# Order of the three matmuls in a block: high weights by low x first, instead of high weights by high x

## The chip, the cores and the metric

The kernel runs on one core of a Trainium2 chip. The metric is the device time of one execution in microseconds (us); lower is better. Before the change the median of three runs is 2578.09 us (2578.03 to 2578.33).

## The reference

The input x has 128 batch elements of 128 channels and 2048 positions (float32). Four layers follow each other, each added to its own input:

```
x = x + conv(x, W0) + (c @ cw0.T)[:, :, None] + side[None, :, None]     # 4 groups, 9 taps, padding 4
x = x + einsum('boi,bih->boh', agg_w1, x) + agg_b1[:, :, None]          # 1x1, weights mixed per batch element
x = x + einsum('boi,bih->boh', agg_w2, x) + agg_b2[:, :, None]          # the same with other experts
x = x + conv(x, W3) + (c @ cw3.T)[:, :, None] + side[None, :, None]     # 4 groups, 9 taps, padding 4
```

Here c is a condition vector of 128 numbers per batch element. For the second and third layer agg_w and agg_b are sums over 8 experts, weighted with a softmax that a small network (two gelu layers) makes of c.

## The kernel before

**Layout.** In a convolution the 2048 positions are cut into 4 phases (PH) of 512 (N). The rows of a tile are then the 32 channels of a group by the 4 phases, and there is one such tile for each of 4 groups (G). Nine taps over 4 phases become BLK = 3 matrices of 128x128, a band with the residual already added on its diagonal. A group of output is thus three column offsets m = 0, 1, 2 of the padded x, each against its own matrix. The two middle layers are joined: their two 128x128 matrices, with their residuals, are multiplied once per batch element (line 917, `middle_matrix`, the short matmuls named `pair<-mixed`), and the product is applied to x in channel rows, phase by phase (`middle`, line 927).

**High and low halves.** float32 accuracy is reached with operands of type float32r in three matmuls. Each operand is split in a rounded high part and the remainder, low. The product is high weights by high x, high weights by low x, low weights by high x, all added in PSUM. I call these three a block. A block stands in `conv` for each (group, m), so 12 blocks for each convolution and batch element, and in `middle` for each phase q, so 4. With two convolutions that makes 28 blocks, 84 big matmuls, for a batch element. The weights of the convolutions (w_hi, w_lo) are made once; m_hi and m_lo are made for each batch element.

**Who makes what.** SyncE issues every transfer in the loop: loads, stores, and the moves between channel rows and phase rows (x_ch, x_ph). ScalarE cuts x in phases, rounds it to x_hi, evacuates PSUM with the bias added (lines 484, 493, 503) and joins the output. VectorE mixes the experts (line 701), makes m_hi and m_lo, and makes the low halves: line 661 for the x of the next batch element, line 752 for the input of the last convolution, group by group (`split_x3`), line 737 for the middle, phase by phase (`split_x1`); lines 654 and 779 do so for the first two elements.

**Order of the work.** Every engine has its order written out by hand. TensorE's loop body for batch element b is `middle_matrix(b)`, `conv1(b)`, `conv4(b - 1)`, `middle(b)`. All waits on semaphores stand ahead of a group (in `conv1` and `conv4`) or of a phase (in `middle`): for the low half of x, which is made after the high half, and for the PSUM bank, which must have been evacuated. Only the last matmul of a group or phase increments a semaphore, with its low weights. The profile's names leave the numbers of tiles out: `x_hi` stands for x_hi, x3_hi and x1_hi, `w_hi` for both layers' weights.

Of the kernel before, what the change touches and what calls it, by code (L numbers as in the profile page):

```python
# [5 lines left out]
def cond_resid_kernel(nc: bass.Bass, a, out):  # L6
# [50 lines left out]
    with ctx:  # L57
        def sb(name, shape, dt=f32):
            return ctx.enter_context(nc.sbuf_tensor(name, shape, dt))
# [12 lines left out]
        x1_hi = sb("x1_hi", [C, PH, N], f32r)  # L72
        x1_lo = sb("x1_lo", [C, PH, N], f32r)
# [11 lines left out]
        w_hi = [sb(f"w_hi{l}", [C, BLK, G, C], f32r) for l in range(2)]  # L85
        w_lo = [sb(f"w_lo{l}", [C, BLK, G, C], f32r) for l in range(2)]
# [6 lines left out]
        m_hi = sb("m_hi", [C, C], f32r)  # L93
        m_lo = sb("m_lo", [C, C], f32r)
# [138 lines left out]
        def wait(eng, s, value):  # L233

            if not (isinstance(value, int) and value <= 0):
                eng.wait_ge(s, value)
# [590 lines left out]
        def _(pe):  # L827
# [23 lines left out]
            for l in range(2):  # L851
# [3 lines left out]
                                 stop=True).then_inc(score_done, 1)  # L855
# [6 lines left out]
            for l in range(2):  # L862
                pe.wait_ge(att_t_ready, l + 1)
                nc.tensor.matmul(bank[2 + l][:, 0:B], bias_k[:, l, :], att_t[l][:, :], start=True,
                                 stop=True).then_inc(bias_l_done, 1)
# [7 lines left out]

            def conv(l, g, hi, lo, done):
                for m in range(BLK):
                    for w, x in ((w_hi, hi), (w_hi, lo), (w_lo, hi)):
                        mm = nc.tensor.matmul(conv_bank[g % 2], w[l][:, m, g, :], x[:, g, m:m + N],  # L877
                                              start=(m == 0 and x is hi and w is w_hi),
                                              stop=(m == BLK - 1 and w is w_lo))
                mm.then_inc(done, 1)  # L880

            def conv1(b, groups=range(G)):
                if not isinstance(b, int) or b >= 2:
                    pe.wait_ge(x_lo_ready, b - 1)
                for g in groups:

                    if isinstance(b, int) and b == 0:
                        pe.wait_ge(x_lo_first, g + 1)
                    if isinstance(b, int) and b == 1:
                        pe.wait_ge(x_lo_second, g + 1)  # L890
                    if g >= 2:
                        pe.wait_ge(x1_ready, G * b + g - 1)
                    elif isinstance(b, int) and b == 1:
                        pe.wait_ge(x1_ready, g + 3)
                    elif not isinstance(b, int) or b >= 2:
                        pe.wait_ge(x4_ready, G * (b - 2) + g + 3)
                    conv(0, g, x_hi, x_lo, conv1_done)

            def conv4(b, groups=range(G), after_x4=False):
                for g in groups:  # L900

                    pe.wait_ge(x3_split, G * b + g + 1)

                    if g >= 2:
                        pe.wait_ge(x4_ready, G * b + g - 1)
                    elif after_x4:
                        pe.wait_ge(x4_ready, G * (b - 1) + g + 3)
                    else:
                        pe.wait_ge(x1_ready, G * (b + 1) + g + 3)
                    conv(1, g, x3_hi, x3_lo, conv4_done)  # L910
# [9 lines left out]
            def middle(b):  # L920

                wait(pe, x3_ready, 2 * b)
                pe.wait_ge(m_split, 2 * b + 2)
                for q in range(PH):
                    pe.wait_ge(x1_split, PH * b + q + 1)
                    for m, x in ((m_hi, x1_hi), (m_hi, x1_lo), (m_lo, x1_hi)):
                        mm = nc.tensor.matmul(mid_bank[:, q, :], m[:, :], x[:, q, :],  # L927
                                              start=(m is m_hi and x is x1_hi), stop=(m is m_lo))
                    mm.then_inc(mid_done, 1)

            def step(b):
                middle_matrix(b)
                conv1(b)
                conv4(b - 1)
                middle(b)
# [18 lines left out]
                             stop=True).then_inc(bias3_done, 1)  # L954

            middle(0)
            conv1(1)
            middle_matrix(1)
            pe.wait_ge(w4_lo_ready, PH)
            conv4(0)  # L960
            middle(1)
            with pe.Fori(2, B - 1) as b:
                step(b)
# [46 lines left out]
```

## Time and profile before

| | |
|---|---|
| median of 3 runs | 2578.09 us |
| the profiled execution, its own time | 2577.78 us |
| its span, first to last instruction | 2575.7 us |
| mean granted TensorE clock | 0.997 |
| TensorE busy, matmuls | 2550.1 us, 99%, 11,068 instructions |
| TensorE weight loads, beside the matmuls | 2069.8 us, 80%, 11,068 |
| VectorE busy | 1955.4 us, 76% |
| ScalarE busy | 2100.5 us, 82% |
| GpSimd busy | 16.1 us, 1% |
| DMA, mean | 314 GB/s |

A busy share says how long an engine had work in it; for TensorE matmuls overlap, each is shown longer than the distance to the next one, so its spacing is read from the starts. The span and the profiled execution's own time differ by what lies around the first and last instruction. The chain that ended last is followed back from the last instruction to what released each piece of work.

### The profile page before, as it was taken

The page shows a single profiled execution, that of the slowest core. Times are in us where ns is not written, and L with a number is a line of the kernel's source. Part 1 is how long each engine was busy: PE and PEld are TensorE (multiplying, and loading weights), DVE is VectorE, ACT ScalarE, POOL GpSimd, SP SyncE. Part 2 cuts the span into 40 slices and gives each one's busy share as a digit, 9 for nine tenths or more (in the row PEclk, how much of TensorE's full clock was granted, in tenths as well). Part 3 has the DMA queues.
Part 4 walks back from the last instruction along what each step waited for, and adds up shares of the span by engine and source line. Part 5 has one row for each costly group of instructions (what it writes and reads, how often), then busy time and mean ns, then how long its engine had stood idle before and what let it go on. Part 6 is the DMA issues. An engine that isn't in the chain of part 4 may idle for free.

```text
span 2575.7 us, 42996 instructions
## 1 busy us (share of the span) xinstructions
PE 2550.1 (99%) x11068; PEld 2069.8 (80%) x11068; DVE 1955.4 (76%) x5032; ACT 2100.5 (82%) x1937; POOL 16.1 (1%) x29
## 2 busy tenths in 40 slices
PE   8999999999999999999999999999999999999998
PEld 6888888888888888888888888888888888888886
DVE  8777777777777777777777777777777777777774
ACT  6888888888888888888888888888888888888885
POOL 2000000000000000000000000000000000000000
PEclk9999999999999999999999999999999999999999
DMA  7888888888888888888888888888888888888876
GB/s 254 316 320 317 318 319 319 315 318 323 318 312 321 323 318 313 320 324 316 315 320 323 315 317 319 322 317 316 320 320 317 317 319 319 316 318 322 317 297 237
DMA packets 334986, 809.31 MB, mean 314 GB/s; under 512 B 37370, under 2 KB 39426, under 8 KB 302210
## 3 DMA queue, kind: packets, MB, share of 16 engines
q1 hardware_dynamic: 332736, 807.69, 84.3%
q10 hardware_dynamic: 2242, 1.53, 0.2%
q8 instruction: 3, 0.05, 0.0%
q14 instruction: 5, 0.04, 0.0%
HBM read 137.97 MB, written 134.23 MB: 106 GB/s over the span
## 4 chain that ended last, share of the span: by engine, by line
PE 98%; DMA 1%; DVE 1%; ACT 0%; SPq 0%; issue 0%; DVEq 0%; ACTq 0%
PE pair L877 82%; PE quad L927 14%; PE pair L917 1%; DMA x_ch<-x_ph 0%; DVE partial L701 0%; DMA mix<-att_saved 0%; DMA x_ph<-in_small 0%; SPq L269 0%; SPq L321 0%; SPq L294 0%; DMA att_saved<-att 0%; ACT x_out L569 0%; ACT x_ch L422 0%; DVE x_hi L734 0%; ACT x_ph L575 0%
## 5 line engine op out<-in xcount | busy, mean ns | idle before, releaser
L877 PE MATMUL pair<-x_hi,w_hi 128*128 128x512 f32 x3072 | 1227.7, 400 | 2.9 <-DVE x_lo L752 1.2
L877 PE MATMUL pair<-x_hi,w_lo 128*128 128x512 f32 x3072 | 1213.5, 395 | 0.0
L877 PE MATMUL pair<-x_lo,w_hi 128*128 128x512 f32 x3072 | 1209.2, 394 | 0.0
L877 PEld LDWEIGHTS pair<-x_hi,w_lo 128*128 128x128 f32 x3072 | 579.7, 189 | 137.5
L877 PEld LDWEIGHTS pair<-x_lo,w_hi 128*128 128x128 f32 x3072 | 582.0, 189 | 131.7
L877 PEld LDWEIGHTS pair<-x_hi,w_hi 128*128 128x128 f32 x3072 | 579.0, 188 | 131.3 <-DVE x_lo L752 1.6
L484 ACT ACTIVATE x_ph<-pair,bias_now 128x512 f32<-128x512 f32 x512 | 351.2, 686 | 254.8 <-PE pair L877 254.7
L422 ACT COPY x_ch<-x_in 128x1024 f32<-128x1024 f32 x255 | 528.3, 2072 | 0.0
L475 ACT COPY x_out<-x_ch 128x1024 f32<-128x1024 f32 x252 | 517.3, 2053 | 0.0
L493 ACT ACTIVATE x_ph<-pair,bias_now 128x512 f32<-128x512 f32 x508 | 355.5, 700 | 191.3 <-PE pair L877 191.3
L734 DVE CAST x_hi<-x_ch 128x512 fp32r<-128x512 f32 x512 | 204.9, 421 | 325.9 <-DMA x_ch<-x_ph 325.9
L701 DVE SCALAR_TENSOR_TENSOR partial<-expert,mix,partial 128x128 f32<-128x128 f32 x1536 | 416.8, 347 | 0.0
L752 DVE TENSOR_TENSOR x_lo<-x_ph,x_hi 128x512 fp32r<-128x512 f32 x512 | 339.9, 684 | 0.0
L737 DVE TENSOR_TENSOR x_lo<-x_ch,x_hi 128x512 fp32r<-128x512 f32 x512 | 339.5, 683 | 0.0
L661 DVE TENSOR_TENSOR x_lo<-x_ph,x_hi 128x2048 fp32r<-128x2048 f32 x126 | 287.6, 2283 | 0.0
L503 ACT ACTIVATE x_ch<-quad,bias_now 128x1024 f32<-128x1024 f32 x256 | 275.4, 1134 | 7.9 <-PE quad L927 7.9
L430 ACT CAST x_hi<-x_ph 128x2048 fp32r<-128x2048 f32 x126 | 239.1, 1898 | 0.0
L748 DVE CAST x_hi<-x_ph 128x512 fp32r<-128x512 f32 x512 | 204.4, 420 | 8.3 <-DMA x_ph<-x_ch 8.1
L927 PE MATMUL quad<-x_hi,m_hi 128*128 128x512 f32 x512 | 203.1, 397 | 2.4 <-DVE x_lo L737 2.4
L927 PE MATMUL quad<-x_hi,m_lo 128*128 128x512 f32 x512 | 203.4, 397 | 0.0
L927 PE MATMUL quad<-x_lo,m_hi 128*128 128x512 f32 x512 | 202.8, 396 | 0.0
L759 DVE TENSOR_SCALAR bias_now<-bias 128x4 f32 (+1 forms) x127 | 21.6, 170 | 150.3 <-ACT x_ph L493 150.3
(83 smaller groups left out, 772.9 us busy)
## 6 DMA issues: line engine op xcount, KB each, us to landing
x_ph<-x_ch SPq DMA_DIRECT2D x1024, 256.0 KB, 2.5
x_ch<-x_ph SPq DMA_DIRECT2D x1024, 256.0 KB, 2.6
x_in<-in_x SPq DMA_DIRECT2D x128, 1024.0 KB, 5.6
out<-x_out SPq DMA_DIRECT2D x128, 1024.0 KB, 4.3
x_out<-in_W SPq DMA_DIRECT2D x8, 144.0 KB, 3.9
expert<-in_e ACTq DMA_DIRECT2D x2, 512.0 KB, 8.1
mix<-att_saved SPq DMA_DIRECT2D x2, 512.0 KB, 6.3
x_ph<-in_small ACTq DMA_DIRECT2D x1, 458.5 KB, 3.4
```

The lines of the kernel that those rows point to most:

```text
L422: nc.scalar.copy(x_ch[:, phases, :], x_in[:, slot, :].rearrange("c (n p) -> c p n", p=PH)[:, phases, :]).then_inc(x_cut, 1)
L430: nc.scalar.copy(x_hi[:, :, HALO:N + HALO], x_ph[:, :, :]).then_inc(x_hi_ready, 1)
L475: nc.scalar.copy(x_out[:, slot, :].rearrange("c (n p) -> c p n", p=PH)[:, phases, :], x4_ch[:, phases, :]).then_inc(x_joined, 1)
L484: nc.scalar.activation(x1_ph[:, g, :], conv_bank[g % 2], ACT.Identity, bias=bias1_now[:, g:g + 1]).then_inc(x1_ready, 1)
L493: nc.scalar.activation(x4_ph[:, g, :], conv_bank[g % 2], ACT.Identity, bias=bias4_now[:, g:g + 1]).then_inc(x4_ready, 1)
L503: nc.scalar.activation(x3_ch[:, phases, :], mid_bank[:, phases, :], ACT.Identity, bias=bias3_now[:, :]).then_inc(x3_ready, 1)
L661: nc.vector.tensor_tensor(x_lo[:, :, HALO:N + HALO], x_ph[:, :, :], x_hi[:, :, HALO:N + HALO].bitcast(f32), ALU.subtract).then_inc(x_lo_re ...
L701: nc.vector.scalar_tensor_tensor(to, term, mix[l][:, b, k:k + 1], of, ALU.mult, ALU.add).then_inc(mix_ready[l], 1)
L737: nc.vector.tensor_tensor(x1_lo[:, q - 1, :], x1_ch[:, q - 1, :], x1_hi[:, q - 1, :].bitcast(f32), ALU.subtract).then_inc(x1_split, 1)
L752: nc.vector.tensor_tensor(x3_lo[:, g - 1, HALO:N + HALO], x3_ph[:, g - 1, :], x3_hi[:, g - 1, HALO:N + HALO].bitcast(f32), ALU.subtract).t ...
L877: mm = nc.tensor.matmul(conv_bank[g % 2], w[l][:, m, g, :], x[:, g, m:m + N], start=(m == 0 and x is hi and w is w_hi), stop=(m == BLK - 1 ...
L927: mm = nc.tensor.matmul(mid_bank[:, q, :], m[:, :], x[:, q, :], start=(m is m_hi and x is x1_hi), stop=(m is m_lo))
```

## The change

In both places where a block is issued, the first two of its three matmuls change places. The flag that starts the accumulation goes to the new first matmul, and the last one (low weights by high x, with the increment) is as before. Nothing else is edited.

```
 for m in range(BLK):
-    for w, x in ((w_hi, hi), (w_hi, lo), (w_lo, hi)):
+    for w, x in ((w_hi, lo), (w_hi, hi), (w_lo, hi)):
         mm = nc.tensor.matmul(conv_bank[g % 2], w[l][:, m, g, :], x[:, g, m:m + N],
-                              start=(m == 0 and x is hi and w is w_hi),
+                              start=(m == 0 and x is lo),
                               stop=(m == BLK - 1 and w is w_lo))
...
 for q in range(PH):
     pe.wait_ge(x1_split, PH * b + q + 1)
-    for m, x in ((m_hi, x1_hi), (m_hi, x1_lo), (m_lo, x1_hi)):
+    for m, x in ((m_hi, x1_lo), (m_hi, x1_hi), (m_lo, x1_hi)):
         mm = nc.tensor.matmul(mid_bank[:, q, :], m[:, :], x[:, q, :],
-                              start=(m is m_hi and x is x1_hi), stop=(m is m_lo))
+                              start=(x is x1_lo), stop=(m is m_lo))
```

## Rows read from the trace of the kernel before

**Rows 1.** The page, busy time, share of the span and instructions per engine.
```profile
PE 2550.1 (99%) x11068; PEld 2069.8 (80%) x11068; DVE 1955.4 (76%) x5032; ACT 2100.5 (82%) x1937; POOL 16.1 (1%) x29
```

**Rows 2.** The page, chain that ended last, by engine and by line.
```profile
PE 98%; DMA 1%; DVE 1%; ACT 0%; SPq 0%; issue 0%; DVEq 0%; ACTq 0%
PE pair L877 82%; PE quad L927 14%; PE pair L917 1%; DMA x_ch<-x_ph 0%; DVE partial L701 0%; DMA mix<-att_saved 0%; DMA x_ph<-in_small 0%; SPq L269 0%; SPq L321 0%; SPq L294 0%; DMA att_saved<-att 0%; ACT x_out L569 0%; ACT x_ch L422 0%; DVE x_hi L734 0%; ACT x_ph L575 0%
```

**Rows 3.** The chain in order of time, 400 to 460 us: start, length, what.
```profile
436.02 2.79 PE quad L927 x12
438.81 0.22 PE pair L917 x2
439.03 16.75 PE pair L877 x72
```

**Rows 4.** The chain's longest pieces over the whole span, first and last steady one.
```profile
419.27 16.75 PE pair L877 x72
...
2494.07 16.75 PE pair L877 x72
```

**Rows 5.** Stretches: length, busy us (instructions), clock, DMA share, GB/s.
```profile
0.00:60.00 60.00, 47.19 (x183) 38.42 (x184) 48.28 (x122) 34.53 (x43) 16.14 (x29) 0.91 0.74 264
...
500.00:1000.00 500.00, 500.00 (x2177) 406.23 (x2176) 383.79 (x996) 414.96 (x380) 0.00 (x0) 1.00 0.86 319
...
38.00:43.00 5.00, 5.00 (x12) 3.89 (x13) 5.00 (x12) 1.11 (x1) 0.00 (x0) 0.50 0.02 3
```

**Rows 6.** Groups of instructions: TensorE's weight loads, one kind of line 877.
```profile
L877 PEld LDWEIGHTS pair<-x_lo,w_hi 128*128 128x128 f32 x3072 | 582.0, 189 | 131.7
```

**Rows 7.** VectorE's instructions in order of time, 990 to 1012 us.
```profile
1004.50 0.68 DVE L737 TENSOR_TENSOR x_lo<-x_ch,x_hi 128x512 fp32r<-128x512 f32 x1
...
1007.65 2.28 DVE L661 TENSOR_TENSOR x_lo<-x_ph,x_hi 128x2048 fp32r<-128x2048 f32 x1
```

**Rows 8.** Instructions of TensorE in order of time, 1008.5 to 1013 us.
```profile
1008.90 0.39 PE L927 MATMUL quad<-x_hi,m_hi 128*128 128x512 f32 x1
...
1011.83 0.47 PE L877 MATMUL pair<-x_hi,w_hi 128*128 128x512 f32 x1
...
1012.14 0.39 PE L877 MATMUL pair<-x_lo,w_hi 128*128 128x512 f32 x1
1012.14 0.19 PEld L877 LDWEIGHTS pair<-x_hi,w_lo 128*128 128x128 f32 x1
1012.37 0.39 PE L877 MATMUL pair<-x_hi,w_lo 128*128 128x512 f32 x1
```

**Rows 9.** Waits of TensorE: us in total, times, longest.
```profile
PE quad L927 <- DVE x_lo L737: 2.4, 2, 1.9
PE pair L877 <- DVE x_lo L752: 1.2, 1, 1.2
PE pair L877 <- DVE x_lo L654: 1.2, 1, 1.2
```

**Rows 10.** Groups of matmuls, 60 to 2500 us: count, busy us, mean ns, idle before.
```profile
L877 PE MATMUL pair<-x_hi,w_hi 128*128 128x512 f32 x2961 | 1181.7, 399 | 0.0
L877 PE MATMUL pair<-x_hi,w_lo 128*128 128x512 f32 x2962 | 1169.0, 395 | 0.0
L877 PE MATMUL pair<-x_lo,w_hi 128*128 128x512 f32 x2962 | 1165.0, 393 | 0.0
L927 PE MATMUL quad<-x_hi,m_lo 128*128 128x512 f32 x496 | 196.2, 396 | 0.0
L927 PE MATMUL quad<-x_lo,m_hi 128*128 128x512 f32 x496 | 195.5, 394 | 0.0
L927 PE MATMUL quad<-x_hi,m_hi 128*128 128x512 f32 x496 | 195.4, 394 | 0.0
```

**Rows 11.** TensorE in order of time, first element's middle, 38 to 43 us.
```profile
38.36 0.63 PE L927 MATMUL quad<-x_lo,m_hi 128*128 128x512 f32 x1
...
42.20 0.63 PE L927 MATMUL quad<-x_lo,m_hi 128*128 128x512 f32 x1
```

## The prediction

> **What bounds the kernel now.** I read the page's busy shares first: TensorE is busy 99% of the span of 2575.7 us, ScalarE 82%, VectorE 76% [rows 1]. The reader should distrust such a share until the chain agrees, so the chain that ended last comes next: 98% of it is TensorE, 82% on the convolutions' line 877, 14% on the middle layers' line 927 and 1% on the matrix product of line 917 [rows 2]. Third, the chain in order of time. In steady state it has three kinds of piece for one batch element and no other: 72 matmuls in 16.75 us, 12 in 2.79 us, 2 in 0.22 us [rows 3]. That is 19.76 us, and the pattern repeats without a drift: from the piece at 419.27 us to the one at 2494.07 us there are 105 batch elements in 2074.80 us, 19.760 us each [rows 4]. No DMA, no ScalarE and no VectorE stands in between.
>
> So the time is a count times a spacing. Per element there are 84 big matmuls (128x512); (16.75 + 2.79) / 84 gives 232.6 ns from one start to the next. The spacing is the same in both places: 16.75 / 72 = 232.6 ns in the convolutions, 2.79 / 12 = 232.5 ns in the middle [rows 3]. Over 128 elements, 84 x 128 = 10,752 matmuls x 0.2326 us = 2501 us, and 128 x 0.22 = 28 us for line 917. The other 47 us of the span are the first and last elements' waits and the start at half clock. The granted clock is 1.00 (the level of 2.4 GHz) in the steady stretch and 0.91 on average in the first 60 us [rows 5].
>
> **The change part by part.** Nothing is removed or added. Within each block of three matmuls the first two change places, in conv 3072 times, in middle 512 times, 3584 blocks in all.
>
> *Count of matmuls and weight loads: 0 us.* The weights run high, high, low in either order, only the moving operand goes from high, low, high to low, high, high. The trace loads weights once for each matmul, also for the second of two that use the same w_hi: 3072 loads on line 877 for the kind shown, and as many for each of the other two [rows 6]; line 927 has 512 of each. There is no skipped reload to lose or to win; 3 x 3584 loads stand on both sides. The loads take 189 ns on average beside a matmul that starts 233 ns before the next one, so they are covered by the stream. Were that cover gone, 189 ns would be to pay per matmul, but the edit lengthens no load.
>
> *The waits: 0 us, and the bound is small.* The first matmul of a block now needs the low half of x, which VectorE makes last. Had the old order let the high matmul start before the low half was there, the change would expose that. It did not: in conv1, conv4 and middle every wait stands ahead of the whole group, and it already is a wait for the low half (x_lo_ready, x3_split, x1_split). Behind it on TensorE is the same group as before. In steady state it binds nowhere. VectorE's line 737 makes the middle's first low phase from 1004.50 to 1005.18 us; TensorE starts the middle at 1008.90, 3.7 us later. Line 661 ends the next element's low x at 1007.65 + 2.28 = 1009.93; conv1 starts at 1011.83, 1.9 us later [rows 7, 8]. TensorE's waits for a low half over the whole trace are 2.4 + 1.2 + 1.2 = 4.8 us, at the two ends [rows 9]. Price 0; the far bound is that these double, +4.8 us, though no instruction that would do it is moved.
>
> *The start flag, the end of a group, the buffers: 0 us.* The start flag moves with the first place. The last matmul is still w_lo by the high x and carries the increment, so evacuations, moves by DMA and the release of x_hi and x_lo come at the same distance from the group's start as before. A third of each block stays where it was; no DMA is issued from TensorE and no queue is passed.
>
> *The pairing of what streams with what is loaded: the one unknown.* Each weight load runs while the matmul before it streams. The rows show it: the load for w_lo starts at 1012.14, in the same hundredth as the matmul with x_lo [rows 8]. Before, high x streams beside a load of w_hi, low x beside w_lo, high x beside the next w_hi. After, low x streams beside w_hi, high x beside w_lo, high x beside the next w_hi. If a step costs something for what streams plus something for what is loaded, the sum over a block is unchanged, since both sets stay (x high, high, low; weights high, high, low). Only an interaction of the two can move the time, and the trace has just the old pairs. Nearest rows: the mean durations of the three kinds between 60 and 2500 us. In conv they are 399, 393 and 395 ns, in the middle 394, 394 and 396 [rows 10]. The 399 holds one matmul in 24 that runs 0.47 us, the first behind line 917, whose two short matmuls leave the next load uncovered [rows 8]; without it the mean is 399 - (470 - 395) / 24 = 396. So the kinds differ by 3 ns in conv and 2 ns in the middle, with another kind the longest. A difference that doesn't stay with the kind doesn't look like a price of a pair. I take 0. For the far bounds one step in each block gains or loses the whole 3 ns: 3584 x 0.003 = 10.8 us either way. For the range I take a third of it, 1 ns per block: 3.6 us.
>
> There is something left to explain in each step. From 38 to 43 us the granted clock is 0.50, the level of 1.2 GHz [rows 5], and nine steps of the middle of the first element take 42.20 - 38.36 = 3.84 us, 426.7 ns each [rows 11]: 512 columns at 1.2 GHz and no more. The same columns at 2.4 GHz are 213.3 ns, but the spacing there is 232.6, 19.3 ns more [rows 3]. Whatever takes these 19.3 ns could depend on the pair, so the rival about pairing stays.
>
> A rule bears on this term. The Trainium skill, "TensorE: Matmul & The Clock Gate", Part 2 (step-by-step), says that TensorE has one read port for the moving operand and another for the weights, so that loading the next weights takes nothing from the running matmul. By it the pairing costs exactly nothing. The same page's Part 1 gives 215.7 ns from start to start for 512 columns at full clock; by it the big matmuls would take 10,752 x 0.2157 = 2319 us. The trace has 232.6 ns and 2501 us for the same matmuls, so the page's two figures do not describe this stream fully.
>
> **Sum.** The profiled execution took 2577.78 us, its span plus 2.1 us around it; 0 + 0 + 0 + 0 leaves it so. It lies 0.31 us (0.01%) under the median of the three runs, 2578.09, so that the forecast is given at the median: 2578.1 us.
>
> **The rivals.** A measurement of this kernel tells about 0.2%, 5.2 us, from no change; that is 1.44 ns per block of three.
>
> *Dearer pairing (slower).* Low x streaming beside w_hi, or high x beside w_lo, costs more than the old pairs. For it: two of three pairs are new, and the kinds do differ by up to 3 ns, and 19.3 ns of each step has no cause that I can name [rows 10, 11]. Against it: the additive argument, and that conv and middle, with other tiles in both roles, run at the same mean spacing. Place: each of 3584 blocks; price at the 3 ns bound +10.8 us, 2588.9 us; it decides from 1.44 ns per block. Chance 8%.
>
> *Cheaper pairing (faster).* The same with the other sign: 2578.1 - 10.8 = 2567.3 us. Chance 6%.
>
> *A repeated moving slice is cheaper.* Now the second and third matmul of a block stream the very same slice of high x. If the second pass saved what lies above 512 columns at 2.4 GHz (213.3 ns), the 19.3 ns, the time would be 3584 x 0.0193 = 69 us less, 2509 us. Against it: in conv the old order already had near-repeats, high x at m behind it high x at m+1, which share 511 of 512 columns, while the middle went on to another phase; yet 232.6 and 232.5 ns are equal. Chance 2%.
>
> *The low half is waited for (slower).* 4.8 us of waits double: 2582.9 us, just under what can be told; beyond it VectorE's halves would have to come 1.9 us later than they do in each element. Chance 2%.
>
> *The change does not do what it says.* The order on the engine might stay as it was; the time is then the forecast's. It is part of the first case.
>
> **How the numbers follow.** Forecast (nothing that can be told) 82%. Dearer pairing 8% and a late low half 2% make slower 10%; cheaper pairing 6% and the repeated slice 2% make faster 8%. The range for 8 in 10 is 1 ns per block either way: 2578.1 +/- 3.6, from 2574.5 to 2581.7 us; it leaves out about 2 in 10, the rivals and the edge of the forecast's own case.
>
> **What would show it.** The changed trace should have 11,068 matmuls and as many loads; the kinds on lines 877 and 927 in the order x_lo with w_hi, x_hi with w_hi, x_hi with w_lo; pieces of 16.75 + 2.79 + 0.22 us in the chain and 19.76 us from one to the next; the mean of 399 moved from x_hi with w_hi to x_lo with w_hi, as that is now the first behind line 917; TensorE's waits for a low half near 4.8 us. A period of 19.84 us or more would mean dearer pairing (28 blocks x 3 ns = 0.08 us), one of 19.68 cheaper pairing, 19.2 a saving on the repeated slice. Wrong would be the argument that the price of a step is a sum of two parts, or the claim that no wait binds in steady state.

## The result and the profile after

The changed kernel takes 2583.74 us (median of 11 runs, 2583.22 to 2586.35) against 2577.61 us before (11 runs, 2576.62 to 2578.33). The ratio is 1.0026 with a 95% interval of [1.0017, 1.0035]: 6.1 us slower, outside the forecast range. The loss is small, but clear of noise.

The chain of the changed kernel in order of time, 1000 to 1062 us (start, length, what), answers to [rows 3]:

```profile
1011.64 2.80 PE quad L927 x12
1014.44 0.22 PE pair L917 x2
1014.66 16.79 PE pair L877 x72
1031.45 2.80 PE quad L927 x12
```

and its longest pieces over the whole span to [rows 4]:

```profile
83.75 16.79 PE pair L877 x72
...
1133.50 16.79 PE pair L877 x72
```

The same three pieces stand there and nothing else, each of the two long ones stretched: 16.79 for 16.75 us and 2.80 for 2.79. From 83.75 to 1133.50 us are 53 batch elements, 19.807 us each, where it was 19.760. I call this the period. 0.047 us x 126 elements is 5.9 of the 6.1 us, so the loss is paid at every element alike. TensorE's waits (total, times, longest) did not change [rows 9]:

```profile
PE quad L927 <- DVE x_lo L737: 2.4, 2, 1.9
PE pair L877 <- DVE x_lo L752: 1.2, 1, 1.2
PE pair L877 <- DVE x_lo L654: 1.2, 1, 1.2
```

The stretch from 500 to 1000 us (PE, weight loads, DVE, ACT, POOL busy, clock, DMA share, GB/s) answers to [rows 5]: the clock is still 1.00, only fewer matmuls fit in, 2172 for 2177.

```profile
500.00:1000.00 500.00, 500.00 (x2172) 404.65 (x2171) 382.77 (x995) 413.62 (x380) 0.00 (x0) 1.00 0.85 318
```

The groups between 60 and 2500 us (count, busy us, mean ns, idle before) answer to [rows 10]:

```profile
L877 PE MATMUL pair<-x_lo,w_hi 128*128 128x512 f32 x2954 | 1177.2, 399 | 0.0
L877 PE MATMUL pair<-x_hi,w_lo 128*128 128x512 f32 x2954 | 1170.4, 396 | 0.0
L877 PE MATMUL pair<-x_hi,w_hi 128*128 128x512 f32 x2953 | 1163.2, 394 | 0.0
L927 PE MATMUL quad<-x_hi,m_hi 128*128 128x512 f32 x496 | 195.4, 394 | 0.0
L927 PE MATMUL quad<-x_hi,m_lo 128*128 128x512 f32 x496 | 195.4, 394 | 0.0
L927 PE MATMUL quad<-x_lo,m_hi 128*128 128x512 f32 x496 | 195.3, 394 | 0.0
```

As foreseen, the 399 went to x_lo with w_hi, the first behind line 917; no kind stands out. The third view, the list of TensorE's matmuls, says where within an element the time went. These are the first matmul of the first convolution, the first of the last convolution (36 later) and the first of the middle (36 later) in one element of the changed kernel:

```profile
1014.42 0.48 PE L877 MATMUL pair<-x_lo,w_hi 128*128 128x512 f32 x1
...
1022.90 0.40 PE L877 MATMUL pair<-x_lo,w_hi 128*128 128x512 f32 x1
...
1031.29 0.39 PE L927 MATMUL quad<-x_lo,m_hi 128*128 128x512 f32 x1
```

The same list of the kernel before:

```profile
1020.28 0.39 PE L877 MATMUL pair<-x_hi,w_hi 128*128 128x512 f32 x1
...
1028.66 0.39 PE L927 MATMUL quad<-x_hi,m_hi 128*128 128x512 f32 x1
```

With the start of that element at 1011.83 [rows 8] the first convolution took 1020.28 - 1011.83 = 8.45 us and the last 8.38; after, 8.48 and 8.39. Three quarters of the loss (0.035 us as the mean of 122 elements, 0.003 in the last convolution, 0.008 in the middle) lie in the first convolution, although both convolutions issue the same 36 matmuls of the same kinds in the same order. They differ in their tiles and in what runs ahead of them: two short matmuls ahead of the first one, the first one itself ahead of the last. The start behind the short matmuls doesn't hold the loss: by the starts in the two traces, the first step went from 313 to 317 ns and the next from 232 to 224 (a step is the time from one big matmul's start to the next one's; means over the same 122 elements). From here on the rival theories were: A, a step's length hangs on where in SBUF the slice and the matrix lie; B, a kind of pair is dear wherever it stands (the prediction's "dearer pairing"); C, the low half is waited for; D, values, or the other engines' reads and writes.

### The profile page after: what moved, and what is told of

It is laid out like the page before. It is cut to its first block, busy times and chain, and to the rows that moved or that the text cites. A ratio compares the mean times of both kernels' runs of the same rounds, so it can differ in the third digit from the quotient of the medians.

```text
span 2581.9 us, 42996 instructions
## 1 busy us (share of the span) xinstructions
PE 2555.9 (99%) x11068; PEld 2066.7 (80%) x11068; DVE 1956.3 (76%) x5032; ACT 2102.8 (81%) x1937; POOL 16.2 (1%) x29
## 4 chain that ended last, share of the span: by engine, by line
PE 98%; DMA 1%; DVE 1%; ACT 0%; SPq 0%; issue 0%; DVEq 0%; ACTq 0%
PE pair L877 82%; PE quad L927 14%; PE pair L917 1%; DMA x_ch<-x_ph 0%; DVE partial L701 0%; DMA mix<-att_saved 0%; DMA x_ph<-in_small 0%; SPq L269 0%; SPq L321 0%; SPq L294 0%; DMA att_saved<-att 0%; ACT x_out L569 0%; ACT x_ch L422 0%; DVE x_hi L734 0%; ACT x_ph L575 0%
## 5 line engine op out<-in xcount | busy, mean ns | idle before, releaser
L877 PE MATMUL pair<-x_lo,w_hi 128*128 128x512 f32 x3072 | 1225.7, 399 | 2.9 <-DVE x_lo L752 1.2
L877 PE MATMUL pair<-x_hi,w_hi 128*128 128x512 f32 x3072 | 1211.0, 394 | 0.0
L430 ACT CAST x_hi<-x_ph 128x2048 fp32r<-128x2048 f32 x126 | 239.6, 1902 | 0.0
```

The costliest lines, as they stand in the source:

```text
L430: nc.scalar.copy(x_hi[:, :, HALO:N + HALO], x_ph[:, :, :]).then_inc(x_hi_ready, 1)
```

## The experiments

All runs but those with TensorE's stream alone compute the whole reference. The period of each is read from two of its longest chain pieces, as above.

**The new order in the first convolution only.**

```
-for w, x in ((w_hi, hi), (w_hi, lo), (w_lo, hi)):
+order = ((w_hi, lo), (w_hi, hi), (w_lo, hi)) if l == 0 else ((w_hi, hi), (w_hi, lo), (w_lo, hi))
+for n, (w, x) in enumerate(order):
```

> The new order stands in the first convolution alone; the last convolution and the middle keep the old one. Between the two traces the 36 big matmuls of the first convolution take 35 ns more per batch element, those of the last one 3 ns more, the middle 8 ns more, 47 ns in all. Theory A (a step's length hangs on where in SBUF the streaming slice and the loaded weights lie, so on this kernel's addresses): the cost stays where it was, 35 ns per batch element, period 19.795 us, about 4.4 us over before, 2582 us. Theory B (a kind of pair, such as low x beside a load of high weights, costs the same wherever it stands): 12 of 28 blocks, 20 ns, period 19.780 us, about 2.5 us over before, 2580 us. Theory C (the low half is waited for): period 19.76 us, TensorE's waits for x_lo grow instead.

The longest pieces of its chain:

```profile
81.96 16.82 PE pair L878 x72
...
1371.13 16.82 PE pair L878 x72
```

65 elements in 1289.17 us: the period is 19.833 us, and the time 2585.55 us (one run, beside 2576.54 before). Both numbers I had for A and B (19.795 and 19.780) are wrong. With 12 of 28 blocks changed the kernel is slower than with all of them. So the parts do not add up: what a convolution costs also depends on what ran just ahead of it. In the list of its matmuls the last convolution, whose order was not touched, takes 8.41 us instead of 8.38:

```profile
1022.38 0.39 PE L878 MATMUL pair<-x_hi,w_hi 128*128 128x512 f32 x1
...
1030.79 0.39 PE L928 MATMUL quad<-x_hi,m_hi 128*128 128x512 f32 x1
```

**Low first, but the old cycle.**

```
-for w, x in ((w_hi, hi), (w_hi, lo), (w_lo, hi)):
+for n, (w, x) in enumerate(((w_hi, lo), (w_lo, hi), (w_hi, hi))):
```

and the same in the middle.

> High weights by low x, low weights by high x, high weights by high x, everywhere. Seen as an endless cycle this is the old order entered one matmul later: the low x comes first, as in the new order, but the pairs of what streams and what is loaded are the old ones but for those across the border of two blocks. Theory B: period 19.76 us, 2577.6 us. A cost of starting a block or a group with the low x: as the new order, 19.807 us, 2583.7 us. Theory A: neither is due; the pairs across the borders have new addresses, so anything within 0.05 us of 19.78 us.

```profile
82.91 16.79 PE pair L878 x72
...
1172.28 16.79 PE pair L878 x72
```

These are the longest pieces of its chain: 55 elements in 1089.37 us, 19.807 us, the period of the changed kernel, and 2583.21 us. That this kernel, with the old pairs of kinds inside a block, lands on the new order's period speaks against B. What it shares with the new order is the sequence of slices that stream: low, high, high. Only the sequence of weights differs (high, low, high for high, high, low). For places that is no difference. w_hi and w_lo of one layer are two tiles of 6144 bytes apart, 12,288 = 48 x 256 bytes, which the next runs show to be nearly the same place. All matrices, m_hi and m_lo too, start at multiples of 256 bytes. So modulo 256 the old and the new order hold the same pairs of slice and matrix, and only their sequence differs. By the starts in the traces this kernel's 84 steps have, position by position, the mean lengths of the changed kernel's to within 0.1 ns, so whether the high or the low weights are loaded made no difference there. It also agrees with a cost of starting with the low x; the moved tiles below exclude that as the whole story.

**TensorE's stream alone.** One big tile covers the addresses of all streaming tiles and matrices; TensorE issues steps from a list of (matrix, slice) addresses, and marks between the stages make each stage's length readable.

```
for name, steps in STAGES:
    for n, (w, x, bank) in enumerate(steps):
        nc.tensor.matmul(pair[:, bank, :], big[:, w:w + 128], big[:, x:x + 512], start=first, stop=last)
    nc.tensor.matmul(pair[:, 0, :], mark[:, 0:128], mark[:, :], start=True, stop=True).then_inc(done, 1)
```

> Not the reference's computation: nothing but big matmuls (128x512, float32r) and their weight loads in a row, one stage after another, with no DMA and no other engine at work and normally distributed values everywhere, at the very SBUF addresses of the kernel. Stages: first convolution, last convolution and middle in old and new order, four other orders, the new and old order with the low x moved by 32 to 2048 bytes, and single slices. Theory A: old and new order of the first convolution differ by 1.0 ns per matmul (232.4 and 233.4 ns), of the last by under 0.2 ns (232.8), and moving the low x by some bytes changes both orders by about as much and with either sign. Theory B: the same difference of 0.55 ns per matmul in all of them and for every move. Theory D (values, or the other engines' reads and writes): no difference between orders here.

The list of TensorE's instructions, merged, for the first convolution in old and in new order, four times 36 steps each; a stage reaches from its start to the next mark:

```profile
45.31 33.76 PE L98 MATMUL pair<-big 128*128 128x512 f32 x144
78.91 0.40 PE L100 MATMUL pair<-mark 128*128 128x512 f32 x1
79.15 33.69 PE L98 MATMUL pair<-big 128*128 128x512 f32 x144
112.68 0.39 PE L100 MATMUL pair<-mark 128*128 128x512 f32 x1
```

(78.91 - 45.31) / 144 = 233.3 ns in the old order, (112.68 - 79.15) / 144 = 232.8 in the new one; for the last convolution it was 233.5 and 232.6, for the middle 233.3 and 233.4. My numbers for A were off again, even in sign, because here each convolution follows itself and not what it follows in the kernel. But B fell, which wanted the new order 0.55 ns slower everywhere: it is the faster one in both convolutions. With low x moved by 64 bytes the orders took 233.5 and 231.8 ns, by 32 bytes 232.8 and 233.1. Both sizes and sign go with the place.

**A sweep of places.**

> Not the reference's computation: as the run with the steps alone, with other places: one streaming slice repeated with one matrix, the slice moved in steps of 32 bytes over 512 bytes and by 0, 4 and 8 more (the column offsets m of the convolution), the matrix moved in steps of 32 bytes, then whole convolutions with all of x moved, with group strides of 2056 and 2304 bytes and others. Theory A, as the run before suggests it: the step hangs on the distance of slice and matrix modulo 256 bytes, so single slices repeat after 256 bytes, the lowest is near 227 ns where the distance is a multiple of 256 (x+128, w+128), the highest near 240 at an offset of 4 bytes; and with a group stride of 2304 the whole convolution follows the single slices, near 229 ns at x+128. Theory E (no order in the places, only the history of a few steps before counts): whole convolutions lie within 1 ns of 233 ns wherever they are.

One slice and one matrix, 48 times each, in the list of TensorE's instructions. These are the stages with the slice at its first place, moved by 4 bytes, by 128, by 196 and by 256; then the matrix moved by 256, and at last both moved by 4:

```profile
46.41 11.36 PE L116 MATMUL pair<-big 128*128 128x512 f32 x48
57.60 0.39 PE L118 MATMUL pair<-mark 128*128 128x512 f32 x1
57.83 11.49 PE L116 MATMUL pair<-big 128*128 128x512 f32 x48
69.15 0.40 PE L118 MATMUL pair<-mark 128*128 128x512 f32 x1
...
184.10 11.06 PE L116 MATMUL pair<-big 128*128 128x512 f32 x48
195.00 0.39 PE L118 MATMUL pair<-mark 128*128 128x512 f32 x1
...
263.83 11.68 PE L116 MATMUL pair<-big 128*128 128x512 f32 x48
275.35 0.40 PE L118 MATMUL pair<-mark 128*128 128x512 f32 x1
...
321.37 11.36 PE L116 MATMUL pair<-big 128*128 128x512 f32 x48
332.56 0.39 PE L118 MATMUL pair<-mark 128*128 128x512 f32 x1
...
687.36 11.30 PE L116 MATMUL pair<-big 128*128 128x512 f32 x48
698.50 0.39 PE L118 MATMUL pair<-mark 128*128 128x512 f32 x1
...
778.33 11.67 PE L116 MATMUL pair<-big 128*128 128x512 f32 x48
789.85 0.39 PE L118 MATMUL pair<-mark 128*128 128x512 f32 x1
```

From start to mark, divided by 48, the slice's places took 233.1, 235.8, 227.1, 240.0 and, 256 bytes on, 233.1 ns again. The whole table, 48 places of the slice, repeats after 256 bytes within 0.2 ns. Moving the matrix by 128 bytes gave 227.7 ns, nearly like moving the slice, and at each of the eight distances in steps of 32 bytes the two ways of moving agree within 0.7 ns. So A held in its core: the same instruction takes 227 to 240 ns, by the places of matrix and slice modulo 256 bytes.

Two readings limit it. First, the distance alone is not enough when the move is small: with slice and matrix both moved by 4 bytes the step took 240.0 ns instead of 233.1, with both moved by 8 bytes 239.6. Second, one pair of places has more than one value. The matrix moved by 256 bytes took 232.1 ns here and 233.3 in the run before. By the starts in the traces, the steps of the one stage soon repeat after seven, from 228 to 241 ns, those of the other are 237 and 229 ns in turn. The instructions are the same; what ran ahead of them was not, nor was the chip. Likewise the order low-high, high-low, high-high, which streams the old order's slices, took 232.3 ns for the old order's 233.3 at the first convolution's places in the run before, and 233.6 for 233.5 at the last one's. A stage's value is thus fixed by its places only to about 1 ns, twice what the edit cost per step.

A's further guess was wrong: with a group stride of 2304 bytes a whole convolution took 232.8 to 234.4 ns, not 229. A sequence of places does not inherit the value of its single places. Theory E, that places don't matter and whole convolutions lie within 1 ns of 233 ns, failed too: over all strides and places they took 231.9 to 235.4 ns. The middle with its x moved by 64 bytes fell from 233.3 to 226.8 ns.

**The middle's x moved in the kernel, both orders.** The first run with this edit has the old order, the second the new one.

```
+sb("gap0", [C, 16])
 x1_hi = sb("x1_hi", [C, PH, N], f32r)
 x1_lo = sb("x1_lo", [C, PH, N], f32r)
+sb("gap1", [C, 48])
```

> The old order; 64 unused bytes ahead of x1_hi and 192 behind x1_lo, so that the streaming tiles of the middle lie 64 bytes further against their matrices modulo 256, and every other pair of tiles as before. Theory A: the middle's step falls as in the sweep, from 233.3 to 226.8 ns, 12 x 6.5 = 78 ns per batch element: period 19.68 us, 2577.6 - 10 = 2568 us. Theory B (kinds of pairs) or any theory in which places don't count: 19.76 us and 2577.6 us.

> The new order with the same 64 and 192 unused bytes. Theory A: the middle falls to about 227 ns per step too, period near 19.73 us, 2583.7 - 10 = 2574 us, faster than the old order at the old places. Theory B: 19.81 us, 2583.7 us.

The old order took 2579.70 us, ratio to before 1.0007 [0.9997, 1.0016], period 19.780 us: the expectation failed. The new order took 2573.41 us, ratio 0.9985 [0.9975, 0.9994], period 19.727 us: it held. At these places the order that was slower by 6.1 us is faster by 2579.70 - 2573.41 = 6.3 us. The chain of the old order (its line numbers are two higher) shows what went wrong with the expectation:

```profile
1008.81 2.74 PE quad L929 x12
1011.55 0.22 PE pair L919 x2
1011.77 16.82 PE pair L879 x72
```

The middle gained 0.05 us, the convolutions behind it, at unchanged distances, lost 0.07 us (16.82 for 16.75). As in the first experiment, steps hand something on to those behind them, and it reaches far. By the starts in the traces the steps here differ from before throughout the first convolution and in the first 13 of the last one, that is for 49 steps behind the middle, and the next 23 are as before within 0.1 ns. In the first experiment too the last convolution differs from before in its first 13 steps and in no other.

**Whole bodies of TensorE's stream alone.**

> Not the reference's computation: only TensorE's stream again, now whole loop bodies (2 short matmuls, first convolution, last convolution, middle) at the kernel's places, three in a row, with the orders old and new mixed, and then a grid of places modulo 256 for the high and low x, in either order. Theory A: without any other engine at work the bodies have the kernel's own periods: old 19.76 us, new 19.81, new in the first convolution alone 19.83; and over the grid the new order is sometimes the faster, sometimes the slower one, by up to 1% of the step. Theory B: the new order is slower at all places by about the same. Theory D (values, or the other engines' reads and writes): all bodies have one period.

The list of TensorE's instructions at the mixed pairs that open a body: new order everywhere (first two rows), new order in the first convolution only (last two):

```profile
124.76 0.38 PE L121 MATMUL other<-big 128*128 128x128 f32 x2
...
144.57 0.38 PE L121 MATMUL other<-big 128*128 128x128 f32 x2
...
184.43 0.38 PE L121 MATMUL other<-big 128*128 128x128 f32 x2
...
204.26 0.38 PE L121 MATMUL other<-big 128*128 128x128 f32 x2
```

19.81 and 19.83 us; the old order's body took 19.76. Each kind runs three times in a row, and these are the second bodies; the first ones, behind other work, differ from them by up to 0.06 us. With the new order in the middle alone it took 19.76 us as well. So the 0.008 us that the middle lost in the kernel came from the convolution ahead of it, not from its own order. These are the kernel's periods, with no DMA, no ScalarE and no VectorE running and with normally distributed numbers in the place of the low halves. D fell. The stream alone also has 19.78 and 19.73 us for the middle moved by 64 bytes, which the kernels had (19.780, 19.727) and my addition of parts had not. Over the grid of 64 places for high and low x a convolution step took 231.3 to 234.0 ns in the old order and 231.3 to 233.9 in the new one, and neither was the better one throughout.

**Two controls: distances kept.** 64 unused bytes ahead of everything that TensorE reads, then 256 bytes ahead of x1_hi.

```
+sb("gap0", [C, 16])      # first run, ahead of x_hi
+sb("gap0", [C, 64])      # second run, ahead of x1_hi
```

> The old order; 64 unused bytes ahead of x_hi, so that every streaming tile and every matrix lies 64 bytes further and no distance between them changes. Theory A as it stands now (only the distance of slice and matrix modulo 256 bytes counts): period 19.76 us, 2577.6 us. Its variant that the places themselves count: another period, off by up to 0.1 us.

> The old order; 256 unused bytes ahead of x1_hi, so that the middle's x, the last convolution's x and all matrices move 256 bytes, the first convolution's x not. Theory A: nothing changes modulo 256, period 19.76 us, 2577.6 us. If unused bytes or the order of tiles as such did something, it would show here.

The periods are 19.760 us in both. For the first run the chain's pieces at 221.87 and 2276.91 us are 104 elements apart:

```profile
221.87 16.75 PE pair L878 x72
...
2276.91 16.75 PE pair L878 x72
```

In both runs all 84 steps have the mean lengths of the kernel before within 0.1 ns. So unused bytes do nothing by themselves, and with moves of 64 and 256 bytes only the distance of slice and matrix counts, which the sweep denies for moves of 4 bytes. The times were 2576.93 us for the second run and 2580.73 for the first, single runs, beside 2577.39; the first lost its 3 us at the end, see below.

**All three moved, both orders.** Unused bytes so that, modulo 256 and against the matrices, the x of the first convolution moves by 96 bytes, that of the middle by 64 and that of the last by 32. These places were among seven tried with the stream alone.

```
+sb("gap0", [C, 24])      # ahead of x_hi
+sb("gap1", [C, 56])      # ahead of x1_hi
+sb("gap2", [C, 56])      # ahead of x3_hi
+sb("gap3", [C, 56])      # ahead of w_hi
```

> The old order, with unused bytes that move, modulo 256 and against the matrices, the first convolution's x by 96, the middle's by 64 and the last convolution's by 32 bytes. TensorE's stream alone had a body of 19.667 us at these places. Theory A: period 19.67 us, (19.667 - 19.760) x 126 = -12 us, 2566 us. Theory B: 2577.6 us.

> The new order at the same places. TensorE's stream alone: 19.593 us. Theory A: period 19.59 us, 21 us under before, 2556 to 2557 us, and 9 us under the old order at these places. Theory B: 2583.7 us.

The old order took 2566.10 us, ratio 0.9958 [0.9944, 0.9972]; the new one 2556.69 us, ratio 0.9918 [0.9902, 0.9935]. The chain of the latter:

```profile
1004.27 16.65 PE pair L881 x72
1020.92 2.72 PE quad L931 x12
1023.64 0.22 PE pair L921 x2
```

The periods are 19.667 and 19.593 us, as the stream alone had them, and the new order is 9.4 us ahead of the old one. At 2556.7 us this version beats the kernel before by 21 us and the changed one by 27.

## Why the prediction was wrong

**What bounds the kernel: right.** A count times a spacing; nothing but TensorE stands in the chain, before and after, and the period alone gives 5.9 of the 6.1 us.

**Weight loads, waits, start flag, buffers at 0 us: right.** 11,068 matmuls and as many loads as before; waits for a low half 4.8 us as before; the low half is not waited for in steady state, so theory C has nothing to stand on.

**The pairing term, 0 with 1 ns per block as its range: this step failed.** It measured 0.047 us / 28 blocks = 1.7 ns per block. Two sentences carried the 0. The first was the additive argument, a price for what streams plus a price for what is loaded, with an interaction of the two as the only way out. Both assume that a step has a price of its own, whatever ran ahead, and the runs show that it hasn't. The last convolution took 8.41 us for 8.38 with only the first one changed. Modulo 256 bytes the edit changes no pair of slice and matrix, only their sequence, and the kernel that swapped the second and third matmul of the new order had the changed kernel's steps. That places set the sizes is shown by the sweep, with 233.1, 227.1 and 240.0 ns for the same matrix and the slice at three places, and by the moved tiles, which turn the sign. The second sentence was "a difference that doesn't stay with the kind doesn't look like a price of a pair". That was true, and it ruled out the wrong thing. The differences belonged not to kinds but to positions in the sequence: in the kernel before the steps behind the first one take from 224 to 240 ns, and group means over 3000 matmuls hide them. The far bound of 3 ns per block did hold the result.

**The rule on the two read ports.** The Trainium skill, "TensorE: Matmul & The Clock Gate", Part 2, has the weight load take nothing from the running matmul, and by it this change costs nothing. The measurement decides against using it here: with the slice left where it was and only the loaded matrix moved by 128 bytes, the step went from 233.3 to 227.7 ns. The sentences in the prediction that called the page's figures incomplete for this stream were right, and I should have given more room to what they left open.

**The rivals.** "Dearer pairing" gave the right sign and, at its bound of 10.8 us, the right order of size; its mechanism, kinds of pairs at 3584 blocks alike, is refuted by the order high-low, low-high, high-high, which came out as slow with the old pairs inside a block, and by the sign that turns with the places. The repeated slice is not cheaper as such: the middle of the changed kernel repeats slices and takes 2.80 us for 2.79.

**What stays open.** Shown was that a step of one repeated pair runs 14 to 27 ns over 213.3 ns, that this depends on the places of slice and matrix modulo 256 bytes, and that what ran ahead counts, for 49 steps in one case. Why was not: a collision of the two reads in SBUF would fit, but is only argued, and so is what carries the history along. No formula here gives the period of a sequence; the stream alone does, by running it. So this case shows what the 6.1 us hang on, the sequence of places in TensorE's own stream, and not what in the chip takes them.

## What to carry to other kernels

Where TensorE's stream is the bound and each matmul loads its own weights, two orders of the same matmuls, or two layouts of the same tiles, can differ by some tenths of a per cent, as here, with nothing in the code to say which is better. Don't credit it to the order: move a tile by 64 bytes and the sign may turn, as it did here. Run TensorE's stream alone at the real addresses, choose places and order together, and judge them in whole bodies, because single steps and single stages do not add up.

## What the runs showed of the hardware that was not expected

- A 128x512 float32r matmul with its own weight load takes 227 to 240 ns from start to start at the granted clock of 1.00, depending on where the slice and the matrix lie modulo 256 bytes. Moving both by 64 bytes changes no step in this kernel; moving both by 4 bytes changed a step from 233.1 to 240.0 ns. At the clock of 0.50 no such excess is seen: 426.7 ns [rows 11].
- In steady state the pattern is free of noise: three kernels with the same distances had the period 19.760 us and the same 84 mean steps within 0.1 ns, and the stream alone had 19.76 us. But a step's length also depends on what ran ahead, in one case for 49 steps.
- The run with everything moved by 64 bytes, same period, took 3 us more at its end. TensorE's list there shows a wait for the middle's first low phase, 1.93 us long, where the kernel before waits 0.49 us at the same matmul. Behind it comes a lowered clock, 0.85 and 0.82 on average in two stretches (columns as in [rows 5]) where the kernel before had 1.00:

```profile
2548.27 0.47 PE L928 MATMUL quad<-x_hi,m_hi 128*128 128x512 f32 x1 [1.93 <-DVE x_lo L738]
...
2546.00:2550.00 4.00, 2.07 (x7) 1.27 (x6) 3.24 (x8) 0.69 (x1) 0.00 (x0) 0.85 0.34 133
2550.00:2556.00 6.00, 6.00 (x23) 4.71 (x23) 0.68 (x2) 2.92 (x3) 0.00 (x0) 0.82 0.12 45
```

The clock is 0.50, the level of 1.2 GHz, for 3.4 us from 2548.8 us on. The longer wait is 1.4 us of the 3, and nine steps at the low clock, 3.67 us for the 2.10 that they take at 233 ns, are the other 1.6. Why VectorE was later there is not known.

So single runs of this kernel can differ by 3 us for a reason that has nothing to do with the period; the period is the better measure of a small change.
